# In the steps that carry expert work, weight loads, two TensorE products and a few VectorE additions change places

## The reference, cut to what matters

```python
x = x + tanh(g_xattn[0]) * L0_xattn(layernorm(x), ctx)
x = x + tanh(g_ffn[0])   * L0_ffn(layernorm(x))          # weights from four bit planes
x = x + tanh(g_xattn[1]) * L1_xattn(layernorm(x), ctx)   # 16 heads of 128
x = x + tanh(g_ffn[1])   * L1_ffn(layernorm(x)[:512 rows])  # 16 experts, top 4
```

```python
q = rmsnorm(xn @ Wq[h]);  k = rmsnorm(ctx @ Wk[h]);  v = ctx @ Wv[h]
out += softmax(q @ k.T / sqrt(128)) @ v @ Wo[h]
```

## Time and profile before

| | |
|---|---|
| median of three runs | 1638.66 us (1632.32 to 1639.54) |
| profiled execution | 1635.06 us, its span 1633.2 us |
| TensorE busy | 1509.5 us, 92% |
| VectorE busy | 1055.8 us, 65% |
| ScalarE busy | 998.0 us, 61% |
| POOL busy | 826.1 us, 51% |
| granted TensorE clock, mean | 0.971 |
| DMA | 138.60 MB moved, mean 85 GB/s |

### The profile page before, as it was taken

How to read it: one execution, slowest core, us unless ns; L and a number is a source line. 1 busy time by engine, 2 the same in 40 slices (tenths; PEclk the granted TensorE clock), 3 DMA queues, 4 the chain that set the end, 5 groups by cost and what they waited for, 6 DMA issues and landing times.

```text
span 1633.2 us, 24699 instructions
## 1 busy us (share of the span) xinstructions
PE 1509.5 (92%) x8506; PEld 1294.5 (79%) x8506; DVE 1055.8 (65%) x2061; ACT 998.0 (61%) x2238; POOL 826.1 (51%) x662
## 2 busy tenths in 40 slices
PE   5889899999999989998999898989998999999997
PEld 3778678888888878887888787878887888878886
DVE  7776656666666756665666565656665666677665
ACT  6864456766775665665666566556665565656654
POOL 3444145555554555555565555555645564663431
PEclk9999879999999999999999999999999999999999
DMA  6310011111111342423243333333333331230002
GB/s 228 127 34 14 1 33 46 40 53 46 40 51 46 118 137 86 137 88 135 86 137 105 118 103 121 108 115 98 126 119 104 112 128 59 84 91 20 20 1 78
DMA packets 53369, 138.60 MB, mean 85 GB/s; under 512 B 5312, under 2 KB 5312, under 8 KB 53248
## 3 DMA queue, kind: packets, MB, share of 16 engines
q1 hardware_dynamic: 49488, 124.71, 23.0%
q0 software_dynamic: 3760, 12.32, 2.9%
HBM read 122.60 MB, written 14.42 MB: 84 GB/s over the span
## 4 chain that ended last, share of the span: by engine, by line
PE 65%; DVE 16%; DMA 6%; ACT 6%; issue 4%; POOL 3%; SPq 0%; ACTq 0%; POOLq 0%; DVEq 0%
PE j_bank L426 8%; PE w_bank L426 8%; PE j_bank L428 8%; PE j_bank L427 8%; PE w_bank L428 7%; PE w_bank L427 7%; PE t_bank L505 5%; DMA cT_raw<-w_gu 3%; DVE x_sb L1221 3%; PE s_bank L426 3%; PE s_bank L428 3%; PE s_bank L427 3%; DMA xnT_raw<-w_gu 2%; ACT prob L806 2%; DVE qT_lo L956 2%
## 5 line engine op out<-in xcount | busy, mean ns | idle before, releaser
L806 ACT ACTIVATE prob<-s_bank,neg_bias,q_scale 128x512 f32<-128x512 f32 x256 | 198.6, 777 | 313.3 <-DVE neg_bias L1182 313.0
L956 DVE TENSOR_TENSOR probT_lo<-t_bank,probT_hi 128x512 fp32r<-128x512 f32 x264 | 179.0, 688 | 211.3 <-ACT probT_hi L708 208.6
L1221 DVE SCALAR_TENSOR_TENSOR x_sb<-w_bank,inv_sum,x_sb 128x512 f32<-128x512 f32 x256 | 187.6, 743 | 12.1 <-PE w_bank L428 12.1
L426 PE MATMUL w_bank<-wo_lo,oT_hi 128*128 128x512 f32 x256 | 117.0, 457 | 69.5 <-DVE x_sb L1221 67.7
L1166 DVE TENSOR_REDUCE neg_max<-s_bank 128x1 f32<-128x512 f32 x256 | 168.8, 679 | 5.9 <-PE s_bank L428 5.9
L505 PE MATMUL t_bank<-ident,prob 128*128 128x128 f32 x1024 | 158.2, 278 | 3.9 <-DVE probT_lo L956 2.0
L1358 POOL TENSOR_TENSOR cT_round<-cT_raw,x_round 128x1408 fp32r<-128x1408 f32 (+1 forms) x31 | 103.8, 3348 | 100.9 <-ACT x_round L708 99.7
L708 ACT CAST probT_hi<-t_bank 128x512 fp32r<-128x512 f32 x264 | 153.4, 595 | 1.6 <-PE t_bank L505 1.6
L426 PE MATMUL j_bank<-wkv_lo,cT_hi 128*128 128x256 f32 x512 | 146.4, 286 | 4.8 <-DVE oT_lo L956 3.4
L428 PE MATMUL j_bank<-wkv_hi,cT_lo 128*128 128x256 f32 x512 | 146.0, 285 | 0.0
L427 PE MATMUL j_bank<-wkv_hi,cT_hi 128*128 128x256 f32 x512 | 145.9, 285 | 0.0
(11 more groups left out here) (241 smaller groups left out, 4585.1 us busy)
## 6 DMA issues: line engine op xcount, KB each, us to landing
stage<-w SPq DMA_DIRECT2D x96, 256.0 KB, 2.6
xnT_raw<-w_gu SPq DMA_DIRECT2D x31, 704.0 KB, 4.1
cT_raw<-w_gu SPq DMA_DIRECT2D x31, 704.0 KB, 4.4
xnT_raw<-w_dn SPq DMA_DIRECT2D x16, 768.0 KB, 4.3
cT_raw<-w_dn SPq DMA_DIRECT2D x15, 768.0 KB, 4.7
planes<-bits SPq DMA_DIRECT2D x16, 512.0 KB, 3.9
y<-stage SPq DMA_DIRECT2D x31, 256.0 KB
x_sb<-x SPq DMA_DIRECT2D x5, 1024.0 KB, 10.4
```

The lines of the kernel that those rows point to most:

```text
L426: pe.matmul(dst, lh, rl, start=first, stop=False)
L806: nc.scalar.activation(prob[:, i, :], s_bank[i % 2][:], ACT.Exp, bias=neg_bias[:, u % 2, i:i + 1], scale=q_scale[:, u % 2, i:i + 1], accum ...
L956: return nc.vector.tensor_tensor(dst, src, hi, ALU.subtract)
L1221: nc.vector.scalar_tensor_tensor(out=here, in0=w_bank[0 if packed else i % 2][:], scalar=inv_sum[:, w % 2, i:i + 1], in1=here, op0=ALU.mul ...
```

## The change

Four edits.

1. Sync engine: from step 16 on the loads of the next head's weights stand behind the down weights of the step, instead of ahead of half 1 (key, query) or ahead of the down weights (output).
2. TensorE, packed steps: `key_turn()` and `project_out(2)` stand before `query((2, 3))` instead of after it. ScalarE splits the turned keys before the query, VectorE makes `key_lo` and `add(2)` before `query_lo`.
3. ScalarE: `query_hi` is cut into `query_hi`, `key_hi` and `query_squares`, the order in steps that aren't packed stays.
4. VectorE, t = 54 to 57: `take(2)` goes behind `probs_lo(0)` and `shift(2)`, `take(3)` behind `shift(3)`.

```diff
             for t in range(NI + 2):
                 b = t - T0
-                if fresh(t):
-                    key_weights(SET[t] + 1)
-                    query_weights(SET[t] + 1)
                 if 0 <= b < NB:
                     gate_up_weights(b, 1, e)
                 if 0 < b <= NB:
                     y_store(b - 1)
-                if fresh(t - 2):
+                if t < H:
+                    key_weights(SET[t] + 1)
+                    query_weights(SET[t] + 1)
+                if 2 <= t < H + 2:
                     out_weights(SET[t - 2] + 1)
...
                 if 0 <= b < NB:
                     down_weights(b, e)
+                if t >= H and fresh(t):
+                    key_weights(SET[t] + 1)
+                    query_weights(SET[t] + 1)
+                if t >= H + 2 and fresh(t - 2):
+                    out_weights(SET[t - 2] + 1)
                 if 0 <= b < NB - 1:
                     e = expert(b + 1)
                     gate_up_weights(b + 1, 0, e)
...
                 probs(2)
                 gate_up(1)
-                query((2, 3))
                 if packed:
                     key_turn()
                     project_out(2)
+                query((2, 3))
+                if packed:
                     turn_inner()
                     probs(3)
                     project_out(3)
...
                     copy_hi(qT[0][:, t % 2, :], j_bank[1][:]).then_inc(q_hi, 1)
+
+                def key_hi():
+                    if not proj:
+                        return
                     need(act, kT_mm, 1, t, 1)
                     nc.scalar.activation(kv[0][:, t % 2, 0, :], t_bank[0][:], ACT.Copy,
                                          scale=gain[:]).then_inc(kT_hi, 1)
+
+                def query_squares():
+                    if not proj:
+                        return
                     need(act, q_lo, 1, t, 1)
...
                 gate_tanh(1)
-                query_hi()
+                if packed:
+                    key_hi()
+                    query_hi()
+                else:
+                    query_hi()
+                    key_hi()
+                query_squares()
                 inner_hi()
                 probs_hi(3)
...
-                for k in range(TOPK - 1):
-                    take(k)
+                take(0)
+                take(1)
                 values_lo()
                 probs_lo(0)
                 maximum(2)
                 shift(2)
-                take(TOPK - 1)
+                take(2)
                 inner(0)
                 values_rows()
...
                 shift(3)
+                take(3)
                 probs_lo(1)
                 if packed:
                     add(1)
                     probs_lo(2)
                     inner(1)
-                    query_lo()
                     key_lo()
                     add(2)
+                    query_lo()
                     inner_lo()
```

## The result

The changed kernel took 1580.18 us (median of four runs, 1578.06 to 1580.61). The kernel before took 1635.49 in the same comparison (1632.3 to 1639.54). The ratio is 0.9658, 95% interval 0.9628 to 0.9688: 3.4% faster. The forecast was 1578 (1560 to 1597). The profiled execution took 1579.88 us against 1635.06, 55.2 us less, where the sum had said 57.5.

What follows compares the result with a forecast made beforehand. TensorE, busy 92%, was taken as the bound, losing time to waits and low clock, mostly in head-change steps. Terms -60 + 4 - 1.5 = -57.5 us from the profiled 1635.06 gave 1577.6, stated as 1578, range 1560 to 1597.

Steps and rivals of the forecast that it cites:

- Part 1: Sync queue: half 1 issued ahead of key and query loads, so head-change steps lose their whole excess; -60 us.
- The low end of the bound: Sync queue term: half 1's landing stays at 7.8 us and 2.8 us of each ScalarE wait remain.
- One sign: Trace after: second gate/up half issued about 5 us after the first score in every step.
- Part 2: TensorE in packed steps: stall moves from project_out(3) to query_squares, round trip 24.97 us against 24.84; +4 us.
- the margin of 1.07 us: Kernel before, packed steps: room between the end of sqs_lo (728.56) and query_squares on TensorE (about 729.63).
- The exps later by 0.7 us, covered: Next step's exps start 0.7 us later against TensorE, covered by ScalarE's idle time before copying the values.
- Part 3: Four steps after the blocks: one VectorE addition less in front removes TensorE's 2.1 us wait for oT_lo; -1.5 us.
- A: Packed steps: the reorder pays too, squares chain has room, step falls to 23.9 us; about 1545 us, chance 0.12.
- B: Half 1 in head-change steps: issued early but lands slowly; +16 us, 1594 us, chance 0.13.
- C: Loads behind down_weights slow the down loads, ScalarE waits and low clock returns; 1650 us, chance 0.05.
- D: Nothing moves: ScalarE's wait is replaced by one of the same length; 1635 us, chance 0.02.
- What it said of the clock: Low clock (1.2 GHz) in head-change steps leaves with the wait; the periods hold it already, nothing added.

Runs made afterwards that it cites:

- e1: Kernel before with only the sync queue's new load order, nothing else changed; 1573.74 us, ratio 0.9646.
- e3: Kernel before with only half 1 issued ahead of the key and query loads, which stay ahead of the down weights; 1573.37 us, ratio 0.9634.
- e8: Kernel before with the key load still first, half 1 second and the query load third; 1574.34 us, ratio 0.9614.
- e7: e1 plus one spare POOL operation of 1.1 us in front of sqs_lo in each packed step; 1577.95 us, ratio 0.9635.
- e6: Changed kernel plus one spare POOL operation of 1.1 us in front of sqs_lo in each packed step; 1668.97 us, ratio 1.0187.
- e10: Changed kernel plus two small spare POOL operations (0.28 us each) in front of sqs_lo in each packed step; 1636.77 us, ratio 1.0019.
- e2: Changed kernel with the sync queue's old loop and the old places of take; 1651.37 us, ratio 1.0127.
- e4: Changed kernel with TensorE's and ScalarE's old order, and on VectorE in packed steps add(2) ahead of key_lo; 1549.06 us, ratio 0.9492.
- e5: Changed kernel with sqs_lo on VectorE instead of POOL in the packed steps; 1564.21 us, ratio 0.9550.
- e9: e1 plus a spare 256 KB copy within HBM right ahead of half 1 in each packed step; 1590.24 us, ratio 0.9746.

## Why the prediction was right

**Part 1, -60.** Measured -58.9 in the marks (e1). The step lengths of the kernel before held it all, the clock's share included, and rows 2 and 3 gave the reason. The change's description has two halves, loads earlier and loads later; e3 and e8 show that only the first matters, as the working had it. The low end of the bound (landings stay at 7.8 us) did not come: the three waits that are left add up to 4.5 us, and the clock is 1.00 from 600 to 1300 us. One sign was given against the wrong event: half 1 goes out 6.3 us after the first score (639.92 to 646.25) and not about 5, because part 2 starts that score 1.0 us earlier. By the marks it is 10.05 to 10.1 in nearly all steps of either kind, where an ordinary step of the kernel before has 9.9. Two readings in the working were off without touching the sum. Of the ten head-change steps four exceed an ordinary one by near 7.8 us, two by near 7 and four by 2.7 to 4.0, not five, two and three; they add up to 60.3. And the excess isn't 7.8 us in every third step: the four short ones are those in which half 1 went to xnT_raw and landed in 4.6 to 4.9 us.

**Part 2, +4.** Measured +5.3 in the marks between e1 and the changed kernel, 6.4 in the medians of two comparisons. The working gave 24.97 a step and it is 25.01. Term by term: squares to last query matmul 20.73 (said 20.68), that to the end of sqs_lo 4.22 (said 4.23), release 0.06. The first of these terms is 0.05 too short. The eight short matmuls in it take 0.91 us behind the stall (642.41 to 643.32) and took 0.80 without one (704.80 to 705.60), which is more than enough for it. e7 tests the margin of 1.07 us and e6 and e10 the claim that the changed kernel has none. The 1.08 us of stall in the working are there too: from the first score to the squares it is 2.49 us (639.92 to 642.41) and was 1.39 (703.41 to 704.80). The row shows 0.82 of it as idle, since idle time is counted from the end of the last score matmul, which is drawn with 0.40 us though the next one would start 0.23 after it, and the first score takes 0.1 longer.

**The exps later by 0.7 us, covered.** It held in the changed kernel: before its copy of the values ScalarE still idles 0.93 us in one step of three and 0.4 in the other two. It was nearer than the working said, which had 1.5 us of idle time in an ordinary step; before the change two steps of three had 0.9. It did not hold with the old queue: there the query load hangs on the same exps (e2). That interaction stood in no term.

**Part 3, -1.5.** The wait of TensorE for oT_lo of 2.1 us is gone. What is left of TensorE's waits from 1380 us on in the changed kernel, one of 0.2 us aside, is this, and all three were there before with nearly the same lengths:

```profile
PE t_bank L510 <- DVE probT_lo L976: 2.0, 1, 2.0
PE t_bank L510 <- ACT prob L812: 1.7, 2, 0.9
PE w_bank L431 <- DVE oT_lo L976: 1.4, 1, 1.4
```

In time it doesn't show. From the last mark to the end it is 288.6 us, and 289.0 in the kernel before; part 1 alone, which keeps the old places of take, has 287.8. One thing that takes it back is in the waits up to 1380 above: in the last packed step key_turn waits 1.4 us for VectorE's probT_lo, which comes with part 2 and was in no term.

```profile
1336.34 0.63 PE L576 MATMUL t_bank<-ident,kv_raw 128*128 128x128 f32 x4 [1.36 <-DVE probT_lo L976]
```

No run takes part 3 by itself, so the -1.5 is neither shown nor refuted.

**The rivals.** A (the reorder pays too, 1545) is refuted by e2 and e6; that something near 1545 can be had, but by another edit, is e4. B (slow landings stay, 1594) is refuted by the trace: the five blocks that landed in 7.1 to 8.2 us are split without a wait. Its counter-argument was misread, though. Ordinary steps did not all write cT_raw in 5.0 us or less; one of them in the kernel before took 6.4 from issue (869.35) to split:

```profile
875.79 1.37 ACT L708 CAST x_round<-cT_raw 128x1408 fp32r<-128x1408 f32 x1 [1.31 <-DMA cT_raw<-w_gu]
```

The half 1 of that block took 6.3 us in e1 and 6.9 in the changed kernel, and that of a later ordinary step (1193.79 to 1200.00 before) 6.2 and 7.3. So these two slow landings come with either order of the queue, and they are most of the 4.5 us of waits that are left. In e5 neither occurs; what makes them stays open. C (slower, 1650) is refuted by the changed kernel itself, in which ScalarE never waits for down weights; e3 has the loads in front of them and loses nothing either. D is refuted by e1.

**What it said of the clock.** It treated the low clock as part of the head-change wait and asked of no other stall whether it would bring it. The changed kernel has a stall of 0.82 us in each packed step in front of nine tenths of a us of tiny matmuls, and by e10 it stands half a us from losing all its gain. The kernel before had a sign of it: in three of its head-change steps (693.58, 854.39 and 1178.81) the clock went to 0.50 after a stall of TensorE of only 2.17 us. The result was right with a risk in it that the range did not hold.

## What to carry to other kernels

In a queue that goes in order, look first for the instruction whose wait comes latest and ask who stands behind it; moving one issue gave all that the larger reshuffle gave. When work is moved ahead of a producer on the busiest engine, add up the whole loop from its last result through the other engines to its next reader, and compare the shift with the margin there: a stall can be moved as easily as removed. When an engine waits for a short operation that stands behind another on a third engine, try that engine's order before the busy one's.

## What the runs showed of the hardware that I had not expected

A stall of TensorE of little over a us can take the clock down, and length alone doesn't decide it. Before the eight matmuls of two columns, a stall of 0.82 us a step left the granted clock at 1.00; with 1.37 it fell, by the step lengths, in 25 of 29 steps and each of them lost 1.5 us; with 1.9 us it fell in 28 of 29 and they lost 1.5 or 3.1.

Before output products, matmuls with 512 columns, longer ones were borne. A stall of 0.82 us left the clock alone in the kernel before and in e1, and e9 has four of 1.25 to 1.85 us with the clock at 1.00 for the 6 us behind each; the longest is the first row below. The ten head-change steps of the kernel before have one long stall each there, of 2.17 (the second row) to 5.8 us. The clock fell behind nine of them, and not behind one of 2.43 us (1340.75).

```profile
784.12 0.50 PE L438 MATMUL w_bank<-wo_lo,oT_hi 128*128 128x512 f32 x1 [1.85 <-DVE x_sb L1233]
```
```profile
693.58 0.51 PE L426 MATMUL w_bank<-wo_lo,oT_hi 128*128 128x512 f32 x1 [2.17 <-DVE x_sb L1221]
```

So the same length of stall had different outcomes in the two places. Whether the short matmuls behind it are what makes the difference was not tested by itself.

A 256 KB copy within HBM ahead of a 704 KB load in the same queue gave ScalarE waits of 1.25 us on the mean in 33 places, whichever of the two areas the load went to; 0.6 us of it is that the load was issued later.
